# A recurrence of sixteen segments and a mixture of experts on one core: the first round begun at position 16 instead of 12

## The reference, cut to what matters

```python
A_bar = expm(dt_A * A)
def step(state, bc):
    b_t, c_t = bc
    s = state @ A_bar + b_t
    s = _layernorm(s, ln_st_g, ln_st_b)
    return (s, c_t * s)
_, ys = jax.lax.scan(step, state0, (Bm, Cm))
ssm = (ys @ D_w.T + D_b) * gate
```

## Time and profile before

| what | value |
|---|---|
| median of 3 runs | 379.48 us (372.4 to 379.49) |
| the profiled execution | 378.27 us |
| its span in the profile | 376.4 us, 1.87 us less |
| TensorE busy | 325.1 us, 86% |
| VectorE busy | 269.8 us, 72% |
| ScalarE, GpSimd busy | 195.3 and 163.0 us |
| mean granted clock of TensorE | 0.92 |

### The profile page before, as it was taken

How to read it: one execution, slowest core, us unless ns; L and a number is a source line. 1 busy time by engine, 2 the same in 40 slices (tenths; PEclk the granted TensorE clock), 3 DMA queues, 4 the chain that set the end, 5 groups by cost and what they waited for, 6 DMA issues and landing times.

```text
span 376.4 us, 11702 instructions
## 1 busy us (share of the span) xinstructions
PE 325.1 (86%) x4052; PEld 249.1 (66%) x4052; DVE 269.8 (72%) x1297; ACT 195.3 (52%) x587; POOL 163.0 (43%) x240
## 2 busy tenths in 40 slices
PE   8599989689788799899899997898999897877970
PEld 7489956676555577677687886676777645665550
DVE  4784697755778677687566664688899765888872
ACT  0238986113333365664566666388876538764210
POOL 6810000177777776777776553444554410000000
PEclk9958999969999589999899998899999989999696
DMA  7999900011511356677566669746574151000102
GB/s 272 199 223 177 174 15 2 0 50 45 203 52 58 112 190 215 215 224 259 180 212 229 232 222 308 253 153 209 196 234 177 60 188 48 30 29 30 48 12 89
DMA packets 44158, 54.81 MB, mean 146 GB/s; under 512 B 6840, under 2 KB 28767, under 8 KB 44095
## 3 DMA queue, kind: packets, MB, share of 16 engines
q1 hardware_dynamic: 37215, 41.46, 37.9%
q0 software_dynamic: 4544, 9.39, 7.8%
q10 hardware_dynamic: 2336, 3.15, 2.7%
HBM read 14.15 MB, written 16.63 MB: 82 GB/s over the span
## 4 chain that ended last, share of the span: by engine, by line
PE 56%; DVE 20%; ACT 8%; issue 7%; ACTq 3%; DMA 3%; POOL 1%; SPq 1%; DVEq 0%; POOLq 0%
PE bank L1130 11%; PE bank L1571 9%; PE bank L1581 6%; PE bank L503 3%; DVE wT L1029 3%; ACTq L594 3%; PE bank L1470 2%; DVE ring L1043 2%; PE bank L1601 2%; PE bank L439 2%; PE bank L1564 2%; PE bank L1549 2%; PE bank L1541 2%; PE bank L1556 2%; DMA token_rows<-rows_out,token_rows_i 2%
## 5 line engine op out<-in xcount | busy, mean ns | idle before, releaser
L1806 POOL DMA_INDIRECT token_rows<-rows_out,token_rows_i x78 | 75.4, 967 | 61.0 <-ACT rows_out L1703 26.6
L1130 PE MATMUL bank<-Mrep,wT 32*32 32x64 f32 x2368 | 66.8, 228 | 16.6 <-DVE wT L1029 16.1
L1130 PEld LDWEIGHTS bank<-Mrep,wT 32*32 32x32 f32 x2368 | 42.4, 108 | 55.1 <-issue 53.1
L1792 POOL DMA_INDIRECT sorted_rows<-late,slots x64 | 62.6, 978 | 19.7 <-issue 14.3
L1696 ACT ACTIVATE desk<-bank,record 128x128 f32<-128x128 f32 x156 | 48.9, 366 | 37.8 <-PE bank L1571 37.5
L1571 PE MATMUL bank<-desk,record 128*128 128x128 f32 x312 | 58.7, 314 | 0.0
L1043 DVE SCALAR_TENSOR_TENSOR ring<-bank,Rho,Dv 128x64 f32<-128x64 f32 x112 | 31.7, 283 | 30.4 <-PE bank L1130 28.5
L1581 PE MATMUL bank<-record,desk 128*128 128x129 f32 x312 | 50.1, 285 | 0.1
L1571 PEld LDWEIGHTS bank<-desk,record 128*128 128x128 f32 x312 | 43.3, 201 | 8.0 <-issue 1.5
L1581 PEld LDWEIGHTS bank<-record,desk 128*128 128x128 f32 x312 | 42.8, 199 | 0.4 <-issue 0.3
L1688 ACT ACTIVATE desk<-bank,cols 128x128 f32<-128x128 f32 x78 | 36.0, 462 | 3.6 <-PE bank L1564 3.6
(11 more groups left out here) (343 smaller groups left out, 640.0 us busy)
## 6 DMA issues: line engine op xcount, KB each, us to landing
record<-experts SPq DMA_DIRECT2D x78, 290.5 KB, 3.0
sorted_rows<-zero_rows SPq DMA_DIRECT2D x2, 2515.5 KB, 28.1
desk<-sorted_rows SPq DMA_DIRECT2D x26, 193.5 KB
pulls<-token_rows SPq DMA_DIRECT2D x8, 516.0 KB, 5.7
X<-in_L_attn_x ACTq DMA_DIRECT2D x4, 512.0 KB, 6.2
out<-xT SPq DMA_DIRECT2D x8, 256.0 KB, 2.0
token_rows<-rows_out,token_rows_i POOLq DMA_INDIRECT x78
experts<-in_L_ffn_ew SPq DMA_DIRECT2D x1, 1024.0 KB, 6.7
```

Of the source, the lines that this page charges most:

```text
L1130: t = pe.matmul(psY[q], wT[q, 32 * c:32 * c + 32], Mrep[q, c, :], start=(c == 0), stop=(c == 1))
L1792: pool.indirect_dma_start(sorted_rows[h], bass.IndirectOffsetOnAxis(ap=slots[:, j, q:q + 1], axis=0), sort_rows[:, q, :], None)\
L1806: pool.indirect_dma_start(token_rows[h], bass.IndirectOffsetOnAxis(ap=token_rows_i[:, g:g + 1], axis=0), rows_out[:, g % OUT_PLACES, :], N ...
```

## The change

`FIRST_STEP` is 16, so round 0 has 16 steps and all rounds together 144 instead of 148; the starting state is computed as before. All tables are counted in t and are written anew: the dense groups keep their places up to step 19 and one more group follows in steps 20 to 23; expert slots begin at step 24, leave out 11 steps (29, 35, ... 89) and then run without a gap to step 115; five C products come in steps 65 to 89 and three in 116 to 118; the sorting scatters end at step 50; mixing starts at 83 and its second half at 121. LAST becomes 112 instead of 116. At the end of rounds 0 to 3 TensorE gets 3 filler matmuls before the boundary product and 5 behind it; from round 1 on they go to bank 6, so that TensorE first waits for ScalarE's last use of that bank. The four pulls of the first half are issued at tiles 43, 48, 53 and 58. The rounds, the test and the redo are otherwise unchanged.

```diff
--- before.py
+++ after.py
@@ -21,7 +21,7 @@
 ROUNDS = 5
 RECORDS = 5
 OUT_PLACES = 5
-FIRST_STEP = 12
+FIRST_STEP = 16
 MAGIC_ROUNDS = 2
 TOLERANCE = 1e-5
 ROOT_TOLERANCE = 4e-4
@@ -1238,23 +1238,24 @@
 
         LAST = STEPS - L
         SLOTS = TILES + 3
-        FIRST_SLOT = 20
+        FIRST_SLOT = 24
+        GAPS = range(29, 90, 6)
         SLOT_AT = {}
         for t in range(FIRST_SLOT, STEPS):
-            if (t - FIRST_SLOT) % 6 != 5 and len(SLOT_AT) < SLOTS:
+            if t not in GAPS and len(SLOT_AT) < SLOTS:
                 SLOT_AT[t] = len(SLOT_AT)
         assert len(SLOT_AT) == SLOTS
         LAST_SLOT = max(SLOT_AT)
-        ABEL_AT = {0: 0, 4: 1, 8: 2, 12: 3, 16: 4, 25: 5, 43: 6, 61: 7}
-        GATE_AT = {1: 0, 5: 1, 9: 2, 13: 3, 17: 4, 31: 5, 49: 6, 67: 7}
-        ROWS_AT = {3: 0, 7: 1, 11: 2, 15: 3, 19: 4, 37: 5, 55: 6, 73: 7}
-        C_AT = {79: 0, 85: 1, 91: 2, 97: 3, 103: 4, 109: 5, 115: 6, 121: 7}
+        ABEL_AT = {0: 0, 4: 1, 8: 2, 12: 3, 16: 4, 20: 5, 29: 6, 47: 7}
+        GATE_AT = {1: 0, 5: 1, 9: 2, 13: 3, 17: 4, 21: 5, 35: 6, 53: 7}
+        ROWS_AT = {3: 0, 7: 1, 11: 2, 15: 3, 19: 4, 23: 5, 41: 6, 59: 7}
+        C_AT = {65: 0, 71: 1, 77: 2, 83: 3, 89: 4, 116: 5, 117: 6, 118: 7}
         SCATTER_LEAD = 12
         SCATTERS_AT = {t: (2, 1, 2, 1, 2)[t % 5] for t in range(20)}
-        SCATTERS_AT.update({t: 1 for t in range(20, 25)})
-        SCATTERS_AT.update({t: 1 for t in range(25, 55) if t % 2 == 0})
+        SCATTERS_AT.update({t: 1 for t in range(20, 29)})
+        SCATTERS_AT.update({t: 1 for t in range(30, 52) if t % 2 == 0})
         assert SCATTER_LEAD + sum(SCATTERS_AT.values()) == 4 * Q
-        MIX_AT = [79, 86, 93, 100, 122, 127, 132, 137]
+        MIX_AT = [83, 90, 97, 104, 121, 126, 131, 136]
         VALUES_PER_STEP = 2
         SUMMED = NB // HALVES
 
@@ -1644,7 +1645,15 @@
                     if n is not None:
                         ssm_product(pe, 0, n)
                     if k == L - 1:
+                        if 0 < r < ROUNDS - 1:
+                            pe.wait_ge(sem("abel_rows"), sum(at <= t for at in ROWS_AT))
+                            if r < 3:
+                                pe.wait_ge(sem("abel"), sum(at <= t for at in ABEL_AT))
+                        if r < ROUNDS - 1:
+                            keep_warm(3, 6 if r else 2)
                         tensor_boundary(pe, turn + 1)
+                        if r < ROUNDS - 1:
+                            keep_warm(5, 6 if r else 2)
                 state_transposes(pe, 0, NB - 1)
                 ssm_product(pe, 0, NB - 2)
                 pe.wait_ge(sem("close_col"), 1)
@@ -1875,9 +1884,9 @@
                         fetch(g + RECORDS)
                     if g % CHUNK == 0 and g // CHUNK + 3 < TILES // CHUNK:
                         load_rows(g // CHUNK + 3)
-                    if g == HALF_TILES + 5:
-                        for n in range(NB // HALVES):
-                            pull(n)
+                    n, behind = divmod(g - HALF_TILES - 4, 5)
+                    if behind == 0 and 0 <= n < NB // HALVES:
+                        pull(n)
                 for n in range(NB // HALVES, NB):
                     pull(n)
                 for n in range(NB):
```

## The result

The changed kernel takes 1858.39 us (median of 4 runs, 1856.32 to 1862.18), the kernel before 378.25 us in the same series (4 runs, 372.4 to 379.49). The ratio is 4.9515 [4.9288, 4.9743]. The prediction was 1835 us. The profiled execution took 1862.18 us, with a span of 1860.2 us.

A forecast was written before the change was run, and what follows sets the result against it. No engine always busy: VectorE's recurrence bounds rounds 0 and 1 (1.55 us a step), TensorE's queue expert-tile steps from round 2. 366.3 us without the redo + 1468 for it = 1834, taken as 1835 us; range 1640 to 2350.

The forecast's parts named there:

- The step that decided: Test after the last round: calculated last difference 1.7e-5 exceeds TOLERANCE 1e-5, so the redo is run; chance 0.86.
- The rival in which the chip's arithmetic moves the difference under 1e-5: Test at the end: it agrees, no redo is run, 366 us, range 361 to 371; chance 0.09.
- The reason given beside it: Round 0: the four steps left out let segments forget a wrong start; one segment converges late.
- The size of the redo: Branch in `fallback`: 16 rounds of 32 steps, 1382 + 66 + 20 = 1468 us, lower bound 1299.
- The step: Redo, VectorE's chain: 1.55 + 0.64 + 0.25 = 2.44 us, with 0.26 for register counts 2.7 us; 1382 us for 512.
- GpSimd's copies of four states at a time lie beside it: Redo steps: GpSimd's copies of states run beside VectorE's chain and add no time.
- Ends of rounds: Redo: boundary with longer root, clearing of `ends` and a first step, 4.1 us x 16 = 66 us.
- The tail: Redo's end: the repeated tail for 8 groups, estimated at 20 us, between 10 and 50.
- The prediction's 7 us: Redo loops: 48 + 16 branches back on VectorE at 108 ns per compare-and-branch, an estimate of 7 us.
- The 144 steps: Program without the redo: changes by rounds together -12 us, span 364.4, time 366.3 us.
- The second rival: Test agrees but fillers don't hold TensorE's clock: 6.7 us lost, 373 to 375 us; chance 0.05.
- third: Redo costs more: 0.13 us per register calculation, 3.5 us a step, 2244 us; inside the range, no separate chance.

The follow-up runs named there:

- a_tol15: The changed kernel with TOLERANCE at 1.5e-5 instead of 1e-5: redo still run, 1861.0 us (one run).
- a_tol20: The changed kernel with TOLERANCE at 2e-5 instead of 1e-5: no redo, 364.62 us, ratio 0.9646.
- the five start positions: The changed kernel with FIRST_STEP 12, 16, 17, 18 or 19, limit 1e-5: 365.97, 1858.39, 361.17, 1857.99 and 365.16 us; redo at 16 and 18 only.
- b_limit_small: The kernel before, start at 12, with TOLERANCE at 5e-7 instead of 1e-5: redo run, 1863.99 us (one run).
- a_ringwait: The changed kernel with VectorE in the redo waiting for GpSimd's copy of the half before last, not the last: 1802.07 us (one run).
- s12_nofill: The changed kernel with start at 12, without the fillers and waits at the ends of rounds: 373.65 us, ratio 0.9844 to the kernel before.
- a_start17: The changed kernel with FIRST_STEP 17, second half of the mixing one step earlier, limit 1e-5: no redo, 361.17 us, ratio 0.9557.
- a_start12: The changed kernel with FIRST_STEP 12 again, all the rest of the change kept: no redo, 365.97 us, ratio 0.9707.
- a_start19: The changed kernel with FIRST_STEP 19, limit 1e-5: no redo, 365.16 us, ratio 0.9681; run again, 365.06 us.

## Why the prediction was right

**The step that decided, shown.** "So `agreed` should be 0, all engines should take the branch": the bracket of a_tol15 and a_tol20, the five start positions and b_limit_small leave nothing else. The rival in which the chip's arithmetic moves the difference under 1e-5 was wrong at 16, and the calculation named the right side in all five positions. The reason given beside it ("The four steps left out are steps in which a segment forgets its wrong start") was too simple: with 17 the calculated difference is 3e-6, with 18 it is 1.5e-5, with 19 6e-6 to 8e-6. So it has to be calculated for each. That one late segment's meeting with the extrapolation decides is what the calculation says; no run shows it.

**The size of the redo: terms that were wrong and cancelled.** Predicted 1468 us; measured 1862.18 - 368.42 = 1494 us between the profiled executions of the changed kernel and a_tol20 (its slowest), and as much between their medians: 26 us or 1.8% more. Its terms by rows:

*The step.* Predicted 2.7 us (2.44 without register counts). VectorE's timeline, an unrolled step and then a step of the loop:

```profile
1002.94 0.24 DVE L1143 STREAM_TRANSPOSE wT<-ring 128x64 f32<-128x64 f32 x1
...
1005.13 0.25 DVE L1143 STREAM_TRANSPOSE wT<-ring 128x64 f32<-128x64 f32 x1
...
1020.83 0.24 DVE L1143 STREAM_TRANSPOSE wT<-ring 128x64 f32<-128x64 f32 x1
1023.15 0.20 DVE L1186 COPY ends<-Dv 128x64 f32 x1 [0.16 <-DVE ring L1146]
1023.38 0.24 DVE L1143 STREAM_TRANSPOSE wT<-ring 128x64 f32<-128x64 f32 x1
```

The 8 unrolled steps of a round need no copy of the drive and take 2.19 us, the 24 in loops 2.54 or 2.55 us. 2.19 is 1.55 + 0.64, the sum made from the earlier trace rows to the hundredth, though the counts of these steps are worked out in registers too: there they are hidden whole. By that sum the steps in loops should take 2.44, so at most 0.1 us a step falls to registers and not 0.26. It stands between the product and the copy, where VectorE's queue has a calculation (ns min/median/max):

```profile
L1186 DVEq FUSED_REGOPS  x384: 64/75/81, 379.1 to 1810.8; - x192
```

A round's steps sum to 8 x 2.19 + 24 x 2.54 = 78.5 us, where 86.4 were predicted: 7.9 us less. (The first step of a round has no root and takes 1.43 us; what is left over below is smaller by the difference.)

*A term that was missing.* "GpSimd's copies of four states at a time lie beside it" was wrong. The copies run beside the steps, but at every fourth step VectorE waits until the copy of the four states just made is done; the query of L1186 in the changed kernel has both waits (us in total, times):

```profile
  POOL Rho L1211: 93.7, 96
  DVE ring L1146: 46.3, 288
```

With 13.1 us more in the unrolled part this is 107 us. The 0.16 us that every copy waits anyhow are in the 2.54 already; without them 91 us are left, 5.7 a round. a_ringwait proves its place, and that 60 us of it can be had.

*Ends of rounds.* What is left of a round is 91.25 - 78.5 - 5.7 = 7.0 us, predicted 4.1. The difference is the return of the outer loop, for which the sum had no term. VectorE's timeline at the end of a round, then the chain that ended last in the same gap, then the DMA queues from 1086.9 to 1090.2 us (packets, MB, share):

```profile
1086.68 0.23 DVE L1195 COPY ends<-bank 128x64 f32<-128x64 f32 x1 [1.31 <-PE bank L1136]
1090.16 0.19 DVE L1170 COPY ring<-ends 128x64 f32<-128x64 f32 x1 [3.25 <-issue]
```

```profile
1087.07 2.88 issue
```

```profile
q14 instruction: 1, 0.01, 1.0%
```

Between the last instruction of a round and the first of the next VectorE stands idle for 3.10 to 3.40 us, at all 15 returns, 48 us together, and waits for nothing that the profile shows; a packet of instructions is fetched in that gap. Without it an end would take a little less than predicted. Together a round was predicted at 90.5 us and took 91.25.

*The tail.* Predicted 20 us. The sixteenth round ends at 1729.1 + 91.25 = 1820.4, so 39.8 us follow, and 4.3 us pass between the verdict and the redo's first instruction (VectorE works on outputs in 3.3 of them), less the 10.3 us that end the span anyway: 34 us. (The sixteenth round has no return behind it, so that some 3 us of it belong to the tail.) TensorE is at half its clock there and the groups go one after the other:

```profile
1843.17 2.08 PE L1471 MATMUL bank<-D_wT,late 128*128 128x128 f32 x8
1845.29 0.69 DVE L1478 SCALAR_TENSOR_TENSOR xT<-bank,gi 128x512 f32<-128x512 f32 x1 [2.71 <-PE bank L1471]
```

By terms, 16 x (-7.9 + 5.7 + 2.9) = +11, and +14 for the tail: the 26 us, to the rounding. The error of 1.8% says little of the terms' quality, and its smallness was luck: the largest single one was off by 126 us, and against it stood two that weren't in the sum, 91 us for GpSimd's copies and 48 for the outer loop's returns.

In a_ringwait one return of a loop of eight steps costs 0.37 us in the stream of VectorE; 32 of them and the 16 entries are 18 us. A return of the outer loop, over a round's whole code, costs 3.1 to 3.4 us in the changed kernel, 48 us for 15 of them, 2.6% of this program. The Trainium skill (Runtime: NRT & Kernel Launch, Instruction fetch mechanics) says that a taken branch whose target isn't in the fetched window waits for a fetch, and names it as one reason why control flow is expensive. The gap with its instruction packet agrees; no run changed the length of the loop to prove it. Both returns cost more than the 108 ns that the Trainium skill, Advanced Engine Details and Errata (Control Flow Timing), gives for a compare-and-branch. The prediction's 7 us by that figure were too little by a factor of nine.

**The 144 steps.** Predicted 366.3 us; a_tol20 took 364.62 in the median and 368.42 in its profiled execution. By rounds, from the same cuts, against the earlier trace rows:

| round | predicted | a_tol20 |
|---|---|---|
| 0 | -6.2 | -7.0 |
| 1 | -2 | -0.4 |
| 2 | -5 | -5.4 |
| 3 | +0.3 | -0.4 |
| 4 and tail | +0.7 | +3.3 |

Round 0 and round 2 were sized rightly. For round 2 the clock's part is shown by s12_nofill. The pull's part is shown for the start at 12 alone: in the changed kernel mixing begins in round 3, so that round 2 is free of its wait in any case. (The 4.85 us of the earlier trace rows are one pull, the one that VectorE waited for, and not four as the prediction read them.) Round 1 gained next to nothing: copies out waited 9.3 us for scatters to land, against 11.0 before, where 2.5 us were to go, and the fillers brought nothing there. The new wait for bank 6 is there too: the boundary of round 1 in the changed kernel, TensorE's timeline,

```profile
175.00 0.81 PE L1602 MATMUL bank<-bias,ones 128*128 128x512 bf16 x3 [0.87 <-ACT xpad L1678]
175.65 0.33 PE L1135 MATMUL bank<-ends,shift 128*128 128x64 f32 x2
176.04 1.24 PE L1602 MATMUL bank<-bias,ones 128*128 128x512 bf16 x5
```

0.87 us of waiting for ScalarE, and 0.81 us of fillers ahead of the product on which VectorE waits (taken as 0.8 and, for the fillers, 0.65). Round 4 was the term with the largest error: TensorE falls to half clock three times in a_tol20's round 4, once in a_start17's, with the same C products and slots ahead of it, as these windows of a_tol20 and of a_start17 show:

```profile
310.00:316.00 6.00, 5.47 (x68) 4.53 (x69) 4.36 (x23) 2.29 (x8) 0.00 (x0) 0.72 0.12 46
...
328.00:334.00 6.00, 6.00 (x72) 4.68 (x64) 3.20 (x17) 3.31 (x11) 0.00 (x0) 0.72 0.13 49
...
340.00:346.00 6.00, 5.94 (x75) 4.57 (x74) 3.56 (x16) 1.91 (x6) 0.00 (x0) 0.83 0.01 3
```

```profile
320.00:326.00 6.00, 4.85 (x64) 4.03 (x65) 5.80 (x25) 2.81 (x11) 0.00 (x0) 0.72 0.11 44
326.00:332.00 6.00, 5.60 (x78) 3.99 (x78) 4.14 (x19) 4.75 (x15) 0.00 (x0) 1.00 0.02 5
```

Round 4 lasts 63.34 us in the one and 59.25 in the other, and 3.6 of the 4.1 us are in three steps (2.72, 3.61 and 4.19 us against 1.67, 2.63 and 2.63). The fillers of the change stand at round ends and don't reach the tail. What makes the clock fall there in one execution and not in another stays open. It isn't the kernel: in four executions of these same 144 steps (the changed kernel, a_tol15, a_tol20, a_ringwait) round 4 lasts 62.7, 59.6, 63.3 and 62.7 us. It is one reason why the four steps are worth 7 us in round 0 and less in the whole, 1.4 us between the medians of a_start12 and a_tol20.

**The second rival** (the clock isn't held) was wrong in its mechanism: the clock was held at the ends of rounds. Of its price of 6.7 us s12_nofill shows the 3.05 in round 2; the 1.14 and 2.28 that it lost in rounds 3 and 4 are within the scatter. The **third** (0.13 us for each register calculation, 3.5 us a step) was wrong: a calculation takes 0.075 us on the queue's row above, and the step 2.19 or 2.54.

## What to carry to other kernels

A path that no row of a profile shows can still decide the time: where a change touches the input of a data-dependent branch, work out the branch's condition from the inputs first, and the schedule second. A numerical margin is not monotone in the size of the shortcut, so each candidate has to be calculated and then run; here 17 kept the limit and saved 4.4% of the time while 16 and 18 lost a factor of five. A sum that comes out right proves the sum and not its terms; check each with its own row. In a loop on an engine look at the gap at each return, and most of all at that of a long outer loop: it can be shown as waiting for nothing.

## What wasn't expected of the hardware

The part ahead of round 0 is the same in all these kernels, yet its first step starts at 80.6 us in some executions and near 86 in others, and TensorE's clock in the first 40 us goes with it. Windows of a_start19 and of a_start17:

```profile
0.00:40.00 40.00, 33.67 (x242) 30.79 (x243) 28.46 (x103) 20.37 (x43) 16.64 (x61) 0.96 1.08 212
```

```profile
0.00:40.00 40.00, 32.60 (x190) 29.45 (x191) 23.50 (x96) 15.10 (x34) 16.61 (x61) 0.79 1.05 212
```

The first step started at 80.61 and 86.46 us; in the kernel before it was 85.31, with a clock of 0.83. What sets the one or the other is open. Those 5 to 6 us are nearly as large as the gap between 372.4 and 379.49 us in the runs of the kernel before, and as large as most effects compared here. So single executions are to be read by rounds from their own first step, and totals by medians and ratios. In the redo the clock is 0.50 throughout: 16 small matmuls every 2.2 to 2.6 us, and nothing else on TensorE, didn't bring it back in 1500 us.
